# Second layer's attention in pairs of heads: scores on bands of 32 rows, four score banks, a new order of the engines

## What is computed

```python
def _L1_xattn_ref(q_tokens, kv_tokens, Wq, Wk, Wv, Wo):
    HEADS = 16
    DK = 128 // HEADS                       # 8
    q = q_tokens @ Wq.T
    k = kv_tokens @ Wk.T
    v = kv_tokens @ Wv.T
    # each reshaped to (batch, head, token, DK)
    attn = jnp.einsum('bhqd,bhkd->bhqk', q, k) * scale
    attn = jax.nn.softmax(attn, axis=-1)
    out = jnp.einsum('bhqk,bhkd->bhqd', attn, v)
    out = out.transpose(0, 2, 1, 3).reshape(B, T_q, Q_DIM)
    return out @ Wo.T
...
x = x + _L1_xattn_ref(_layernorm(x, axis=-1), ctx_768, L1_xattn_Wq, L1_xattn_Wk, L1_xattn_Wv, L1_xattn_Wo)
```

## Time and profile before

| | |
|---|---|
| median of 3 runs | 1843.81 us (1841.55 to 1843.93) |
| the profiled execution | 1845.27 us, its span 1843.5 us |
| TensorE (PE) busy | 1555.6 us, 84% of the span |
| VectorE (DVE) busy | 1148.8 us, 62% |
| ScalarE (ACT) busy | 871.1 us, 47% |
| GpSimd (POOL) busy | 346.2 us, 19% |
| mean granted TensorE clock | 0.936 |

### The profile page before, as it was taken

The page is one execution under the profiler, slowest core; times in us unless marked ns, Lnnn a source line. Parts: engine busy times, 40 slices in busy tenths (PEclk is TensorE's granted clock), DMA queues, the critical chain, the costliest instruction groups (busy, mean ns, idle before and its releaser), DMA issues.

```text
span 1843.5 us, 38645 instructions
## 1 busy us (share of the span) xinstructions
PE 1555.6 (84%) x13108; PEld 1149.8 (62%) x13108; DVE 1148.8 (62%) x2843; ACT 871.1 (47%) x1860; POOL 346.2 (19%) x657
## 2 busy tenths in 40 slices
PE   4989999979998879997447177999977999999977
PEld 3667777756665668886235054666655767776765
DVE  4867777765666668887301246555544877777761
ACT  1656565543342557776135043233313656556642
POOL 2000000101110323331120605100000122222221
PEclk9999999989999889999579579999996999999999
DMA  9200000000000300000011020000000000000000
GB/s 262 62 2 0 0 0 0 0 1 1 1 0 0 95 1 0 0 0 2 6 49 36 23 54 1 1 1 1 0 0 0 2 1 0 0 0 0 0 1 23
DMA packets 32088, 28.86 MB, mean 16 GB/s; under 512 B 6058, under 2 KB 26419, under 8 KB 31812
## 3 DMA queue, kind: packets, MB, share of 16 engines
q1 hardware_dynamic: 30980, 25.66, 4.8%
q0 software_dynamic: 1024, 2.10, 0.4%
HBM read 21.52 MB, written 6.23 MB: 15 GB/s over the span
## 4 chain that ended last, share of the span: by engine, by line
PE 61%; DVE 15%; issue 10%; ACT 6%; POOL 5%; DMA 1%; SPq 1%; DVEq 0%; POOLq 0%; ACTq 0%
PE bank L1456 52%; PE bank L1460 9%; DVE negm L2180 2%; DVE PTs L2194 2%; DVE negm L2183 2%; DVE Qz L2467 2%; DVE VxF L726 1%; ACT Pm L1298 1%; ACT Pm L1417 1%; ACT Pm L1381 1%; POOL yn L968 1%; DVE st L1993 1%; POOL token_rows_by_expert L1176 1%; ACT PTs L1256 1%; POOL Qz L1185 1%
## 5 line engine op out<-in xcount | busy, mean ns | idle before, releaser
L1298 ACT ACTIVATE Pm<-bank,negm 128x256 f32<-128x256 f32 x784 | 322.2, 472 | 325.7 <-DVE negm L2183 213.6
L1456 PE MATMUL bank<-kT,Qz 64*128 64x256 f32 (+2 forms) x1568 | 296.1, 402 | 3.7 <-issue 1.3
L2194 DVE TENSOR_TENSOR PTs<-bank,PTs 128x512 f16<-128x512 f32 x384 | 251.4, 683 | 33.2 <-ACT PTs L1256 31.8
L1460 PE MATMUL bank<-ident,Pm 128*128 128x128 f32 x1568 | 226.1, 280 | 38.8 <-DVE PTs L2194 30.9
L1456 PE MATMUL bank<-xHL,R 128*128 (+3 forms) x1008 | 235.4, 381 | 13.4 <-DVE Qz L2467 13.3
L1460 PEld LDWEIGHTS bank<-ident,Pm 128*128 128x128 f32 x1568 | 174.1, 142 | 107.3 <-issue 73.6
L1456 PEld LDWEIGHTS bank<-kT,Qz 64*128 64x128 f32 (+1 forms) x1568 | 182.1, 188 | 73.5 <-issue 57.9
L2183 DVE TENSOR_REDUCE negm<-bank 128x2 f32<-128x512 f32 x264 | 176.5, 687 | 79.4 <-PE bank L1456 76.7
L1256 ACT ACTIVATE PTs<-bank 128x512 f16<-128x512 f32 (+1 forms) x388 | 218.6, 604 | 3.0 <-PE bank L1460 3.0
L1417 ACT ACTIVATE Pm<-bank,upback 128x512 f32<-128x512 f32 x168 | 115.3, 687 | 199.1 <-PE bank L1456 198.8
L2467 DVE SCALAR_TENSOR_TENSOR Qz<-bank,upback,Pm 128x512 f32<-128x512 f32 x168 | 124.6, 749 | 115.6 <-ACT Pm L1417 114.1
(11 more groups left out here) (269 smaller groups left out, 1886.8 us busy)
## 6 DMA issues: line engine op xcount, KB each, us to landing
token_rows_by_expert<-wpad SPq DMA_DIRECT2D x10, 256.0 KB, 4.3
R<-in_L_ffn_ew SPq DMA_DIRECT2D x2, 1024.0 KB, 7.1
R<-in_L_ffn_w SPq DMA_DIRECT2D x1, 2048.0 KB, 9.9
R<-in_L_xattn_Wkv SPq DMA_DIRECT2D x2, 768.0 KB, 6.4
Qz<-token_rows_by_expert SPq DMA_DIRECT2D x23, 64.0 KB, 1.9
expert_rows<-Qz SPq DMA_DIRECT2D x23, 64.0 KB, 1.5
R<-in_L_ffn_w SPq DMA_DIRECT2D x1, 1408.0 KB, 12.4
R<-in_L_xattn_Wq SPq DMA_DIRECT2D x2, 512.0 KB, 4.0
```

The source lines that it names most:

```text
L1298: last = act.activation(Pm[:, k % 4, qt * S:(qt + 1) * S], bank[k % 2][:, qt * S:(qt + 1) * S], ACT.Exp, bias=negm[:, k % 4, qt:qt + 1])
L1456: return pe.matmul(o, l, r, start=start, stop=stop)
L1460: return pe.transpose(o, i, ident[0:n, 0:n])
L2194: dve.tensor_tensor(PTl[:, k % 4, :], bank[2 + k % 2][:, :], PTh[:, k % 4, :], ALU.subtract).then_inc(s.pt[1].sem, 1)
```

## The change

The second layer's attention works in pairs of heads.

- **Masks.** `quadmask` has four columns; column j is the sum of the head masks j, 4+j, 8+j and 12+j, so it leaves one head in each band of 32 partitions. GpSimd masks the queries four times per batch, 256 columns each, into `Qz[:, 0..3, :]`, and copies the batch's keys into `Qz[:, 4, :]` (`keys`). The keys, last in GpSimd's order, wait for all scores of the batch before, and the first scores of a batch wait for the keys.
- **Scores.** `pair8`: the two heads of a pair lie on two neighbouring bands of 32 rows (bands 0 and 1 for even pairs, 2 and 3 for odd ones); their matmuls alternate between the bands. `narrow_head` gives the head that stands at a place in this order.
- **Banks.** Scores use banks 0 to 3, transposes 4 and 5, values the halves of bank 6, fills the halves of bank 7. A value product now waits for the normalisation of the pair before.
- **Order.** `narrow_steps(p)` lists a pair's step as the engines meet it: low, low, pair8, max, max, exp, exp, av, av, turn, turn, norm; `softmax` is parted into `max` (VectorE) and `exp` (ScalarE), one step later. The fills stand after steps 1, 3 and 6. In the last batch the splits stand at the end of steps 1 to 4, two each, as in the first layer.

```diff
-NARROW = {4: [("outT", -1)], 7: [("wo", 0), ("resid", 0)], 13: [("ln", 0), ("turns", 0)]}
+NARROW = {1: [("outT", -1)], 3: [("wo", 0), ("resid", 0)], 6: [("ln", 0), ("turns", 0)]}
...
-def head_steps(i):
-    st = [("scores", i), ("softmax", i)] if i < 16 else []
-    st += [("turn", i - 2)] if i < 18 else []
-    st += [("low", i - 3)] if i < 19 else []
-    st.append(("av", i - 4))
-    if i % 2:
-        st.append(("norm", (i - 4) // 2))
+def narrow_steps(p):
+
+    a, b = 2 * p, 2 * p + 1
+    st = [("low", a - 4), ("low", b - 4)]
+    if p < 8:
+        st += [("pair8", a), ("max", a), ("max", b)]
+    if p < 9:
+        st += [("exp", a - 2), ("exp", b - 2)]
+    st += [("av", a - 4), ("av", b - 4)]
+    if p < 9:
+        st += [("turn", a - 2), ("turn", b - 2)]
+    st.append(("norm", p - 2))
     return st
+
+
+def narrow_head(k):
+
+    p, u = k % 16 // 2, k % 2
+    return 4 * (2 * (p % 2) + u) + p // 2
...
-    for i in range(A.nh):
-        st += [(kind, k) for kind, k in head_steps(i) if k >= 0 or not first]
-        st += [step for step in NARROW.get(i, []) if kept(step)]
+    for p in range(8):
+        st += [(kind, k) for kind, k in narrow_steps(p) if k >= 0 or not first]
+        st += [step for step in NARROW.get(p, []) if kept(step)]
+        if last and 1 <= p:
+            st += [("split", i) for i in range(2 * p - 2, min(2 * p, UP_BLOCKS[1]))]
...
+        def fill_bank(A, kinds, m):
+
+            if A.n == 1 and kinds not in ("early", "prologue"):
+                return bank[7][:, 256 * (m % 2):256 * (m % 2) + 256]
+            return bank_of(m)
+
+        def score_bank(A, k):
+
+            return bank[2 * (k // 2 % 2) + k % 2] if A.n == 1 else bank[k % 2]
+
+        def turn_bank(A, k):
+
+            return bank[4 + k % 2] if A.n == 1 else bank[2 + k % 2]
+
+        def value_part(A, p):
+
+            if A.n == 1:
+                return bank[6][:, 256 * (p % 2):256 * (p % 2) + 256], 64
+            return bank[4 + p % 2][:, :], P
...
+            link(pool.tensor_tensor(quadmask[:, :], headmask[:, 0:4], headmask[:, 4:8], ALU.add))
+            link(pool.tensor_tensor(quadmask[:, :], quadmask[:, :], headmask[:, 8:12], ALU.add))
+            link(pool.tensor_tensor(quadmask[:, :], quadmask[:, :], headmask[:, 12:16], ALU.add))
...
                         pool.tensor_tensor(
-                            Qz[:, h:h + 4, :], xnT[:, bass.ts(bw, S)].unsqueeze(1).to_broadcast([P, 4, S]),
-                            headmask[:, h:h + 4].unsqueeze(2).to_broadcast([P, 4, S]), ALU.mult).then_inc(s.qm.sem, 1)
+                            Qz[:, h // 4, :], xnT[:, bass.ts(bw, S)],
+                            quadmask[:, h // 4:h // 4 + 1].to_broadcast([P, S]), ALU.mult).then_inc(s.qm.sem, 1)
+
+                def keys(b, bw):
+
+                    if b is not None:
+                        need(pool, s.scores, b * 16 + 16)
+                    plain(pool)
+                    pool.tensor_copy(Qz[:, 4, :], kTall[:, bass.ts(bw, S)]).then_inc(s.qm.sem, 1)
...
                     if A.n == 1 and kinds == "mid":
                         masks(b, b + 1, (8, 12))
+                        keys(b, b + 1)
...
-                            if A.n == 1 and kinds == "last" and 0 <= k - 4 < UP[A.n][2]:
...
+                        elif kind == "pair8":
+                            if k == 0 and kinds == "first":
+                                fills_read(b, m)
+                            if k % 4 == 0:
+                                need(pe, s.qm, b * 5 + 5)
+
+                            need(pe, s.exp, b * nh + (k - 2))
+                            for qt in range(2):
+                                for u in range(2):
+                                    g = 2 * (k // 2 % 2) + u
+                                    rows = slice(32 * g, 32 * g + 32)
+                                    last = mm(score_bank(A, k + u)[:, qt * S:(qt + 1) * S],
+                                              Qz[rows, k // 4, qt * P:(qt + 1) * P],
+                                              Qz[rows, 4, :])
+                                    if qt == 1:
+                                        last.then_inc(s.scores.sem, 1)
...
-                                    need(pe, s.norm, b * 8 + (p - 1))
-
+                                    need(pe, s.norm, b * 8 + (p if A.n == 1 else p - 1))
```

More of the change, by code:

```diff
@@ L220, in att_epilogue @@
     st = []
-    for i in range(16, 20):
-        st += [(kind, k - 16 if kind != "norm" else k - 8) for kind, k in head_steps(i)]
+    for p in (8, 9):
+        st += [(kind, k - 16 if kind != "norm" else k - 8) for kind, k in narrow_steps(p)]
     return st + [("outT", -1), ("wo", 0), ("resid", 0)]
@@ L1037, in body @@
                         need(pool, s.ring.act, 5)
+                        need(pool, s.ring.dve, 4)
                         masks(None, 0)
+                        keys(None, 0)
                         return
@@ L1054, in body @@
                         masks(0, 1)
+                        keys(0, 1)
                     if A.n == 1 and kinds == "mid":
@@ L1578, in fill @@
                     bw = 0 if kinds in ("early", "prologue", "single") else b if own_fill(A, (kind, k)) else b + 1
-                    need(pe, s.ring.dve if m % 2 else s.ring.act, b * (per // 2) + m // 2)
+                    if A.n == 1 and kinds not in ("early", "prologue"):
+                        fills_read(b, m)
+                    else:
+                        need(pe, s.ring.dve if m % 2 else s.ring.act, b * (per // 2) + m // 2)
                     if kind == "q" and A.dh == 64:
@@ L1654, in body @@
                                         last.then_inc(s.scores.sem, 1)
+                        elif kind == "pair8":
+                            if k == 0 and kinds == "first":
+                                fills_read(b, m)
+                            if k % 4 == 0:
[10 more added lines that the diff above has]
+                                        last.then_inc(s.scores.sem, 1)
                         elif kind == "scores":
-                            if k == 0 and kinds in ("single", "first"):
+                            if k == 0:
                                 fills_read(b, m)
-                            if A.n == 1 and k % 4 == 0:
-                                need(pe, s.qm, b * 4 + (k // 4 + 1))
                             need(pe, s.exp, b * nh + (k - 1))
@@ L1674, in body @@
                                 for qt in range(2):
-                                    last = turn(bank[2 + k % 2][:, kt * S + qt * P:kt * S + (qt + 1) * P],
+                                    last = turn(turn_bank(A, k)[:, kt * S + qt * P:kt * S + (qt + 1) * P],
                                                 Pm[:, k % 4, qt * S + kt * P:qt * S + (kt + 1) * P])
@@ L1691, in body @@
                                 if k % 2 == 0:
-                                    need(pe, s.norm, b * 8 + (p - 1))
+                                    need(pe, s.norm, b * 8 + (p if A.n == 1 else p - 1))
+                                o, step = value_part(A, p)
+                                h = narrow_head(k) if A.n == 1 else k % 16
                                 for qt in range(2):
@@ L1698, in body @@
                                         for n, (pp, vv) in enumerate(((PTh, VxH), (PTh, VxL), (PTl, VxH))):
-                                            last = mm(bank[4 + p % 2][:, r * P:r * P + A.dh + 1],
+                                            last = mm(o[:, r * step:r * step + A.dh + 1],
                                                       pp[:, k % 4, kt * S + qt * P:kt * S + (qt + 1) * P],
-                                                      Vhead(A, b if k >= 0 else b - 1, kt, k % 16, vv), kt == 0 and n == 0,
+                                                      Vhead(A, b if k >= 0 else b - 1, kt, h, vv), kt == 0 and n == 0,
                                                       kt == 1 and n == 2)
@@ L2156, in body @@
                             values_scale_and_ones(A)
-                        if A.n < 2 and kinds == "first" and kind == "softmax" and k >= 4:
+                        if A.n < 2 and kinds == "first" and kind in ("softmax", "max") and k >= 4:
                             t, lo, blocks = UP[A.n]
```

61 lines of the change are left out of this document (25 added, 36 removed).

## The result

The changed kernel takes **1921.26 us** (median of 4 runs, 1920.5 to 1922.65) against 1843.87 for the kernel before, run beside it. The ratio is 1.0403, with a 95% interval from 1.0386 to 1.0421. Forecast were 1830 and a range of 1813 to 1849. The profiled execution took 1922.65, its span is 1920.9 against 1843.5.

What follows compares the result with a forecast made beforehand. TensorE was taken as the present bound, a loop through three engines as the next. First batch 3.6, middle batches 16.6, last batch -6.0 and drain -0.1 gave 14 us less: 1830 us against 1843.81, range 1813 to 1849.

Steps and rivals of the forecast that it cites:

- the clock falls in the steady stretch: Rival for the middle batches: TensorE's clock drops, 4.8 us a pair, 95 us over the forecast, 1925; chance 4%.
- The pair's slot: TensorE's time for two heads' scores on 32-row bands: 1.07 us instead of 1.74, taken from the first layer's 64-row pair.
- rival of serial bands: Rival for the scores: bands run one after the other, pair 1.96 us, 16 us more, 1860; chance 12%.
- The loop, 3.1 us a pair: Second layer's attention: a chain through VectorE, TensorE and ScalarE, once per step, sets 3.1 us a pair.
- a longer loop: Rival for the pair's step: 0.2 us a step lost to unseen waits, 11 us in all, 1841; chance 10%.
- The batch: A steady batch of 16 heads: 8 x 3.1 + 1.8 = 26.6 us, 2.8 less than 29.37.
- The residual's +1.6: Fill after step 3: the residual holds VectorE 1.43 us and delays the next low part from 3.1 to 4.7.
- the fills of step 6: Layer-norm transposes after step 6 of each batch: said to fit in TensorE's gap, no cost.
- GpSimd: Masks and keys' copy: mask 0.48 to 0.73 us, hidden; at the stage's start 0 to 1.8, taken as 0.
- The first batch: Stage's first batch: VectorE-bound at 3.92 us a pair, ending in an all-reduce stall 3.6 us ahead of before.
- The last batch: Batch with eight weight splits: four steps of 6.5 to 7.4 us, 41.3 in all, 6 more than now.
- The sum: Whole kernel: 3.6 + 16.6 - 6.0 - 0.1 = 14 us less, giving 1830; chance 62%.

Runs made afterwards that it cites:

- rows64: The change with a pair's scores on two bands of 64 rows (heads p and 8+p) instead of 32, eight masks; 1860.26 us, ratio 1.0068.
- before32: The kernel before, old order and banks, with each head's scores alone put on bands of 32 rows, one after the other; 2040.02 us, ratio 1.1046.
- filler2: The change plus two full-array products of 512 columns per pair ahead of its scores, which overwrite their results; 1865.98 us, ratio 1.0091.
- rows64_turns7: rows64 with the dummy transposition that closes a batch's fills moved from step 6 to step 7; 1850.77 us, ratio 1.0024.
- full_both: full_rows with the dummy transposition in step 7 and the last batch's splits one at the end of each step; 1849.37 us, ratio 1.0018.
- rows64_three: rows64_split2 with the residual cut in three parts on VectorE, in steps 3, 4 and 5; 1830.12 us, ratio 0.9891.
- rows64_split2: rows64_turns7 with the last batch's splits one per step, behind the exponentials (ScalarE) and maxima (VectorE); 1837.5 us, ratio 0.9932.
- full_rows: The change's order and banks, with scores over all 128 rows and sixteen masked query copies as before; 1857.64 us, ratio 1.0056.
- change_three: The change with its 32-row bands plus the dummy-transposition, split and residual edits of rows64_three; 1867.32 us, ratio 1.0089.
- filler1: The change plus one full-array product of 512 columns per pair ahead of its scores; 1915.55 us, ratio 1.0345.

## Why the prediction was wrong, point by point

**The step that failed is the weighing of the rival "the clock falls in the steady stretch", at 4%.** The forecast took TensorE at 1.00 through the middle batches; measured were 0.56 in 700 to 730 and 0.50 in 820 to 850. The rival gave 4.8 us a pair and 1925; measured were 4.55 and 1921.3. That the totals meet is in part luck. The rival put 95 us on the clock alone; the bands, with the clock that they lose, cost 62 (1.0403 against 1.0068). The other 30 or so are what rows64 too lies above the forecast (1860.26 against 1830): the terms below that were mis-sized. I argued against a fall of the clock with how much of TensorE's time is transposes and gaps, from a stretch whose scores fill all 128 rows. What the change alters, products over a quarter of the rows, was weighed for its slot and not for the clock. The row that could have warned is the earlier trace rows's second: the first layer, too, had pauses and a clock of 0.73. And the prediction itself had gaps behind the residual and four split steps of 3.4 us in which the clock falls; it took for granted that it returns. The Trainium skill, TensorE: Matmul & The Clock Gate, Part 1: The HAM clock gate, What's actually happening, has the clock follow how busy the engine has been recently. By busy share alone the trace doesn't agree: before32 is busy 30.00 of 30 us at 0.50.

**The pair's slot.** 1.07 was right for 32 rows at full clock. filler2 shows it in its timeline (its window from 730 to 760 has clock 1.00):

```profile
742.33 0.59 PE L1494 MATMUL bank<-mb,identb 128*128 128x512 bf16 x2
742.73 1.29 DVE L2253 TENSOR_TENSOR PTs<-bank,PTs 128x512 f16<-128x512 f32 x2 [0.43 <-ACT PTs L1304]
742.86 1.13 PE L1494 MATMUL bank<-Qz 32*128 32x256 f32 x8
...
743.92 0.99 PE L1494 MATMUL bank<-VxF,PTs 128*128 x24
...
744.78 1.06 PE L1498 MATMUL bank<-ident,Pm 128*128 128x128 f32 x8
```

Scores 742.86 to 743.92 = 1.06, value products 0.86 (0.82 forecast), transposes to 745.68 = 0.90 (0.86). Bands overlap, so the rival of serial bands is out. No extra cost of changing from 128-row products to 32-row bands shows in it: 1.06 against the 1.07 of the first layer's 64-row pair. At half clock the slots are 2.01, 0.66 and 1.88.

**The loop, 3.1 us a pair**, is 3.33 from 739.53 to 742.86 in filler2, 3.34 in rows64_turns7, 3.37 in full_both. In filler2 and full_both TensorE's slots fill the step (filler2: 0.53 + 1.06 + 0.86 + 0.90 = 3.35), so TensorE is the bound there. rows64_turns7 has no fillers and nearly the same step, so there the loop is. Its links:

```profile
793.24 1.29 DVE L2247 TENSOR_TENSOR PTs<-bank,PTs 128x512 f16<-128x512 f32 x2 [0.55 <-ACT PTs L1301]
...
794.16 1.24 PE L1491 MATMUL bank<-VxF,PTs 128*128 x24
...
795.26 1.06 PE L1495 MATMUL bank<-ident,Pm 128*128 128x128 f32 x8
...
795.93 1.09 ACT L1301 ACTIVATE PTs<-bank 128x512 f16<-128x512 f32 x2 [0.78 <-PE bank L1495]
...
796.56 1.29 DVE L2247 TENSOR_TENSOR PTs<-bank,PTs 128x512 f16<-128x512 f32 x2 [0.53 <-ACT PTs L1301]
```

Both low parts 1.29 (1.28 forecast), transposes to copy 0.67 (0.66), copy to the next low part 0.63 (0.63). The term that was mis-sized lies between: from the end of low(b), 794.53, to the next transposes are 0.73 us, and in filler2, from 744.02, 0.76, where I had 0.07 + 0.41 = 0.48. The two value products take 1.10 in this row (794.16 to 795.26), where I had 2 x 0.41, so the first isn't done when low(b) ends: b's matmuls start at 794.75. It isn't that one stands directly behind the other: at half clock the same two took 0.66 (878.34 to 879.00). In the last batch of rows64, before the splits begin, the same way takes 0.37 (840.76 to 841.13) and the step 2.97 (pairs at 839.16 and 842.13). In the traces some of the matmuls of a product start 0.12 apart in the middle batches of rows64_turns7, but 0.025 apart in that last batch. Why was not tried. So the rival "a longer loop", 0.2 a step, at 10%, is what rows64_turns7 shows; in the changed one the clock covers it.

**The batch.** 26.6 forecast; 39.4 measured on average over five; 28.8 in the best batch of rows64_turns7 and 27.9 in rows64_three, which is 8 x 3.33 + 1.3. The residual's +1.6 was right (a step of 4.70 instead of 3.34 in rows64_turns7, 784.89 to 789.59: 1.4). Missed was the wait of the dummy transposition for ScalarE's copy, 8 us over the stage: two fills in a row now share bank 7, and I costed the fills of step 6 at nothing.

**GpSimd.** Mask 0.61 and keys' copy 0.40, hidden in the middle of the stage, inside the bounds of 0.48 and 0.73. At the start I took 0 of a range of 0 to 1.8 for the five operations that scores now wait for, and 0 it was. The first scores stand at 617.25 instead of 615.45, but TensorE's last operation ahead of them already came 1.80 later, at 616.26 instead of 614.46. GpSimd's copy of the keys ends at 616.46, before ScalarE's read at 616.57, which came 1.81 later too.

**The first batch.** VectorE's 3.92 a pair is what rows64 has at full clock (low parts at 627.33, 631.23, 635.12: 3.90). In the changed kernel the half clock made each step 4.55. The all-reduce comes at 652.99, 2.3 later than before, where the stall behind it was to end 3.6 earlier.

**The last batch.** 41.3 forecast, 45.1 between the output projections of the last two batches in the changed kernel. Steps with two splits were to take 6.5 to 7.4 us, and one of them takes 7.12, at half clock (value products at 905.13 and 912.25):

```profile
905.13 1.08 PE L1494 MATMUL bank<-VxF,PTs 128*128 128x9 f16 x24 [2.07 <-DVE PTs L2251]
...
912.25 1.08 PE L1494 MATMUL bank<-VxF,PTs 128*128 128x9 f16 x24 [2.22 <-DVE PTs L2251]
```

TensorE's pause is 2.1 to 2.4 us in each, where I had 3.4; its own work in the step is at half clock. The mechanism was the one named, one engine's split waiting for the other's with the low parts behind it. What was not seen is that it could be had for less: the edit in rows64_split2 gained 17 us.

**The sum.** Of the 14 us hoped for, rows64_three has 20, by edits that the change doesn't have: bands of 64 rows and three moves in the queues.

## What to carry to other kernels

A change of a matmul's shape is a change of TensorE's clock until a run shows otherwise: look for the granted clock of a stretch with that shape before adding up slots, and price a pause by what the clock does after it, not by its own length. In an order written out by hand, every step that waits for another engine belongs behind the ready work of its own queue; three such places were worth 8 us (the dummy transposition), 17 (splits) and 8 (residual) here. And when a program has lost the clock, adding work can make it faster: two products a pair whose results nobody reads gained 55 us.

## What the runs showed of the hardware that I had not expected

- TensorE busy 30.00 of 30 us and granted 0.50 all the same, through 700 to 730 us in before32, where each head's scores cover 32 rows; 1.00 in the kernel before, in the same order, and in full_rows, where they cover 128.
- Two stable levels in one and the same loop with 32-row scores: 63 us at 1.00 and 51 us at 0.50 in change_three. Its runs, from 1851.47 to 1890.93, spread more than those of any other kernel here; next is filler1, 1899.85 to 1929.96.
- At full clock 32 rows bring nothing over 64 here: change_three and rows64_three both take 27.9 us a batch (797.00 to 824.92, and 778.47 to 806.39).
